# A gated linear attention block: the part of the state carried in as quarter-array products added in PSUM, and x normalised and turned a tile ahead

## The reference

```python
h = layernorm(x) * (1 + ca) + sa
q, k, v = h @ Wq.T, h @ Wk.T, h @ Wv.T          # 16 heads of 64
log_decay = -softplus(h @ Wd.T + bd)            # one number a token and head
k = k * sigmoid(h @ Wg.T)
s_t = exp(log_decay_t) * s_{t-1} + k_t^T v_t ;  o_t = q_t s_t
x = x + ga * (rmsnorm(o) * norm_w * sigmoid(h @ Wog.T)) @ Wo.T
h = layernorm(x) * (1 + cb) + sb
x = x + gb * ffn(h)                             # token shift, sigmoid(r) * (relu(k)^2 @ Wv)
```

## Time and profile before

| | us |
|---|---|
| median of 3 runs | 3521.03 |
| lowest, highest | 3518.96, 3521.23 |
| the profiled execution | 3524.34 |
| its span in the trace | 3522.6 |
| PE busy in it | 3429.8 (97%) |
| DVE, ACT, POOL busy | 1938.0, 1235.5, 436.6 |
| first pass, from the first transposes of x to the last sum o | 43.5 to 2181.4 |

### The profile page before, as it was taken

The page is one execution under the profiler, slowest core; times in us unless marked ns, Lnnn a source line. Parts: engine busy times, 40 slices in busy tenths (PEclk is TensorE's granted clock), DMA queues, the critical chain, the costliest instruction groups (busy, mean ns, idle before and its releaser), DMA issues. The chain is left out here.

```text
span 3522.6 us, 83072 instructions
## 1 busy us (share of the span) xinstructions
PE 3429.8 (97%) x30085; PEld 3140.0 (89%) x30085; DVE 1938.0 (55%) x4693; ACT 1235.5 (35%) x3072; POOL 436.6 (12%) x723
## 2 busy tenths in 40 slices
PE   7999999999999999999999997899999999999998
PEld 7999999999999999999999996799989899899987
DVE  4444444444444444444444444667677766767676
ACT  4334334333333333333333332332333333233332
POOL 0110110110110110110110111212111111112110
PEclk8999999999999999999999997899999999999999
DMA  4333332332332333333333324422221122212220
GB/s 146 94 95 74 99 91 74 102 87 75 104 85 75 106 83 76 106 82 76 105 82 80 103 75 126 147 72 82 77 91 71 71 83 91 76 71 77 77 95 24
DMA packets 243936, 309.08 MB, mean 88 GB/s; under 512 B 22160, under 2 KB 188064, under 8 KB 239792
## 3 DMA queue, kind: packets, MB, share of 16 engines
q1 hardware_dynamic: 243888, 308.42, 29.7%
HBM read 223.40 MB, written 84.93 MB: 88 GB/s over the span
## 5 line engine op out<-in xcount | busy, mean ns | idle before, releaser
L730 DVE SCALAR_TENSOR_TENSOR mid<-state,w_cur,psQ 64x64 f32<-64x64 f32 x512 | 143.4, 280 | 686.0 <-PE psQ L525 682.3
L627 ACT ACTIVATE prob<-cum_rows,w_cur 128x128 f32<-128x128 f32 x1024 | 327.4, 393 | 132.2 <-POOL cum_rows L808 105.0
L55 PE MATMUL psJ<-h_hi,w_g_hi 128*128 128x256 f32 x1024 | 311.0, 304 | 21.7 <-DVE h_lo L686 20.9
L55 PE MATMUL psJ<-h_hi,w_q_hi 128*128 128x256 f32 x1024 | 303.9, 297 | 0.0
L607 ACT COPY q<-psJ 128x256 f32<-128x256 f32 x256 | 95.8, 374 | 586.6 <-PE psJ L57 586.6
L55 PE MATMUL psG<-h_hi,w_og_hi 128*128 128x256 f32 x1024 | 287.1, 280 | 7.0 <-DMA h_lo<-h_dram 7.0
L56 PE MATMUL psJ<-h_lo,w_q_hi 128*128 128x256 f32 x1024 | 285.4, 279 | 0.0
L56 PE MATMUL psJ<-h_lo,w_g_hi 128*128 128x256 f32 x1024 | 285.3, 279 | 0.0
L57 PE MATMUL psJ<-h_hi,w_g_lo 128*128 128x256 f32 x1024 | 284.7, 278 | 0.0
L55 PE MATMUL psJ<-h_hi,w_k_hi 128*128 128x256 f32 x1024 | 284.0, 277 | 0.7 <-ACT w_new L613 0.7
L57 PE MATMUL psJ<-h_hi,w_q_lo 128*128 128x256 f32 x1024 | 284.6, 278 | 0.0
(11 more groups left out here) (214 smaller groups left out, 9656.8 us busy)
## 6 DMA issues: line engine op xcount, KB each, us to landing
cum_rows<-cum_dram SPq DMA_DIRECT2D x256, 256.0 KB, 5.6
grown<-cum_dram SPq DMA_DIRECT2D x512, 64.0 KB, 3.4
o_dram<-o SPq DMA_DIRECT2D x256, 128.0 KB, 1.9
o_cols<-o_dram SPq DMA_DIRECT2D x32, 1024.0 KB, 5.9
an_norm_x<-in_L_attn_x_dram SPq DMA_DIRECT2D x32, 512.0 KB, 3.5
h_dram<-h_hi SPq DMA_DIRECT2D x32, 512.0 KB, 4.0
h_dram<-h_lo SPq DMA_DIRECT2D x32, 512.0 KB, 5.2
h_hi<-h_dram SPq DMA_DIRECT2D x32, 512.0 KB, 3.9
```

The lines of the kernel that those rows point to most:

```text
L55: nc.tensor.matmul(out, w_hi, x_hi, start=first, stop=False)
L627: last = nc.scalar.activation(prob[:, p % 2, 2 * h + c, :], cum_rows[:, p % 4, 2 * c + h, :], ACT.Exp, bias=w_cur[:, 0, c, 2 * p + h:2 * p ...
L730: last = nc.vector.scalar_tensor_tensor(out=mid[r, r], in0=state[r, p, r], scalar=w_cur[r, 3, 0, 2 * p + h:2 * p + h + 1], in1=psK[r, 0, r ...
```

## The change

The output of a pair is now summed in PSUM. `grow_q` (DVE) multiplies q with `grown` before the product, `weigh_v` opens the sum with prob times v, and `add_held`, one step later, adds the products of the grown q with the state before the first chunk (`held`, a copy by ACT) and with `mid`, in four matmuls of 64x64 quarters of the array. The full-array products with state and mid, `inter` and the sum `add_o` are gone; ACT copies the finished o out of PSUM (`copy_o`). State and mid are 128x64, and DVE updates each in one instruction with one scalar a row (`w_all`). In psO the two chunks of a pair lie crosswise over the partitions, so o is stored with four DMAs of 64x128 in place of one of 128x256. psK moved into the bank of the scores and psN into psO's.

x is loaded in step 1 for two tiles ahead, normalised in steps 4 and 5 of the tile before, turned in step 1 (before the pair's k), and scaled in step 2; `rest_h` makes its four pieces in a row. The loop over tiles is one tile shorter, with that tile written out.

```diff
-        state = sb("state", [P, NP, P])
-        mid = sb("mid", [P, P])
+        state = sb("state", [P, NP, DH])
+        held = sb("held", [P, 2, DH])
+        mid = sb("mid", [P, 2, DH])
-        inter = sb("inter", [P, NC, CH])
+        qg = sb("qg", [P, 2, T])
...
-        psS, psX, psN = psB[:, :, 0:2, :], psB[:, 0, 2:4, :], psB[0:2 * NC * H, 1, 2, :]
-        psQ = ps("psQ", [P, 4, CH])
-        psI, psK = psQ[:, 0:2, :], psQ[:, 2:4, :]
-        psO = ps("psO", [P, 4, CH])[:, 0:NC, :]
+        psS, psX, psK = psB[:, :, 0:2, :], psB[:, 0, 2:4, :], psB[:, 1, 2:4, 0:DH]
+        psP = ps("psP", [P, 2, 4, CH])
+        psO, psN = psP[:, :, 0, :], psP[0:2 * NC * H, 0, 1, :]
...
         def grow_rows(sp, i, p):
-            hold(sp, s["inter"], NP * i + p - 1)
+            hold(sp, s["qg"], NP * i + p - 1)
...
         def sp_tile(sp, i, gla, proj, prep):
             j = i - 1
-            if prep:
-                hold(sp, s["xT"], KD * (i + 1))
-                sp.dma_start(x[:, :, :], x_v[i + 1]).then_inc(s["x"], 16)
             for p in range(NP):
+                if p == 1 and prep > 1:
+                    sp.wait_ge(s["xT"], KD * (i + 2))
+                    sp.dma_start(x[:, :, :], x_v[i + 2]).then_inc(s["x"], 16)
...
                     sp.wait_ge(s["o"], NP * j + p + 1)
-                    sp.dma_start(o_v[j, :, p, :, :], o[:, p % 2, :, :]).then_inc(store[p % 2], 16)
+                    for h in range(2):
+                        for side in range(2):
+                            sp.dma_start(o_v[j, h * DH:(h + 1) * DH, p, (h + side) % 2, :],
+                                         o[side * DH:(side + 1) * DH, p % 2, h, :]).then_inc(store[p % 2], 16)
...
         def weigh_v(pe, n, p):
             pe.wait_ge(s["prob"], n + 1)
+            pe.wait_ge(s["mid"], n + 1)
+            pe.wait_ge(s["held"], n + 1)
+            pe.wait_ge(s["qg"], n + 1)
             hold(pe, s["o"], n)
...
+                    side = (h + c) % 2
+                    nc.tensor.matmul(psO[side * DH:(side + 1) * DH, h, :], v[:, c, p * P + h * DH:p * P + (h + 1) * DH],
+                                     prob[:, p % 2, 2 * h + c, :], start=True, stop=False, tile_position=(0, side * DH))
+
+        def add_held(pe, p):
+            for c, s_in in enumerate((held, mid)):
+                for h in range(2):
+                    r, side = slice(h * DH, (h + 1) * DH), (h + c) % 2
+                    last = nc.tensor.matmul(psO[side * DH:(side + 1) * DH, h, :], s_in[r, p % 2, :],
+                                            qg[r, p % 2, c * CH:(c + 1) * CH], start=False, stop=True,
+                                            tile_position=(h * DH, side * DH))
             last.then_inc(s["gla"], 1)
...
+                if p == (1 if gla else 4) and prep:
+                    turn_x(pe, i + 1)
...
-                    nc.tensor.matmul(psI[:, 0, :], state[:, p, :], q[:, p, 0:CH], start=True,
-                                     stop=True).then_inc(s["held"], 1)
+                    if p > 0 or not opens:
+                        add_held(pe, (p - 1) % NP)
...
-                if gla:
-                    pe.wait_ge(s["state"], n + 1)
...
-                    nc.tensor.matmul(psI[:, 1, :], mid[:, :], q[:, p, CH:T], start=True,
-                                     stop=True).then_inc(s["ready"], 1)
...
-                if p == 6 and prep:
-                    turn_x(pe, i + 1)
...
+        def keep_state(act, j, p):
+            n = NP * j + p
+            hold(act, s["state"], n + 1 - NP)
+            hold(act, s["gla"], n - 1)
+            nc.scalar.copy(held[:, p % 2, :], state[:, p, :]).then_inc(s["held"], 1)
+
+        def copy_o(act, n, p, j):
+            act.wait_ge(s["gla"], n + 1)
+            hold(act, store[p % 2], 64 * (NP // 2 * j + p // 2))
+            nc.scalar.copy(o[:, p % 2, :, :], psO[:, :, :]).then_inc(s["o"], 1)
...
-                if p == 7 and prep:
+                if p == (2 if gla else 5) and prep:
                     affine_h(act, i + 1)
...
-        def add_o(dve, n, p, j):
-            dve.wait_ge(s["gla"], n + 1)
-            dve.wait_ge(s["inter"], n + 1)
-            hold(dve, store[p % 2], 16 * (NP // 2 * j + p // 2))
-            nc.vector.tensor_tensor(o[:, p % 2, :, :], inter[:, :, :], psO[:, :, :], ALU.add).then_inc(s["o"], 1)
+        def grow_q(dve, j, p):
+            n = NP * j + p
+            dve.wait_ge(s["by_act"], act_done(j, ("q", p)))
+            dve.wait_ge(grow[p % 2], 32 * (NP // 2 * j + p // 2 + 1))
+            hold(dve, s["gla"], n - 1)
+            nc.vector.tensor_tensor(qg[:, p % 2, :], q[:, p, :], grown[:, p % 2, :, :].rearrange("p c t -> p (c t)"),
+                                    ALU.mult).then_inc(s["qg"], 1)
...
+                    grow_q(dve, j, p)
+                    dve.wait_ge(s["score"], n + 1)
                     dve.wait_ge(s["held"], n + 1)
...
+                    nc.vector.scalar_tensor_tensor(out=mid[:, p % 2, :], in0=state[:, p, :], scalar=w_all[:, 0, p:p + 1],
+                                                   in1=psK[:, 0, :], op0=ALU.mult, op1=ALU.add).then_inc(s["mid"], 1)
                     dve.wait_ge(s["mid"], n + 1)
...
-                    for k in range(2 if gla else KD):
+                    for k in range(KD):
                         rest_h(dve, i, k)
...
-                if p == 4 and prep:
-                    norm_stats(dve, i + 1)
-                if p == 5 and prep:
-                    norm_x(dve, i + 1)
+                if p == 4 and prep > 1:
+                    norm_stats(dve, i + 2)
+                if p == 5 and prep > 1:
+                    norm_x(dve, i + 2)
```

More of the change, by code:

```diff
@@ L360, in attention_pass @@
         s = signals(nc, ctx, "a", "xT hT h_hi h_lo h_kept zb softin e1 l soft g_raw cum w_new n_turned n_out n_rows "
-                 "cur proj by_act k e mask score prob kT kw inc mid state held ready gla inter o zero")
+                 "cur proj by_act k e mask score prob kT kw inc mid state held qg gla o zero")
         s.update(norm["s"])
@@ L430, in _ @@
         def _(sp):
[L431 to L436, removed]
+            sp.wait_ge(s["xT"], KD)
+            sp.dma_start(x[:, :, :], x_v[1]).then_inc(s["x"], 16)
+            sp_tile(sp, 0, False, True, 2)
+            sp_tile(sp, 1, True, True, 2)
+            with sp.Fori(2, NT - 2) as i:
+                sp_tile(sp, i, True, True, 2)
+            sp_tile(sp, NT - 2, True, True, 1)
+            sp_tile(sp, NT - 1, True, True, 0)
+            sp_tile(sp, NT, True, False, 0)
             for n in range(2):
-                sp.wait_ge(store[n], 16 * NP // 2 * NT)
+                sp.wait_ge(store[n], 64 * NP // 2 * NT)
             sp.wait_ge(s["h_kept"], 32 * NT)
@@ L474, in weigh_v @@
                 for h in range(2):
-                    last = nc.tensor.matmul(psO[h * DH:(h + 1) * DH, c, :],
-                                            v[:, c, p * P + h * DH:p * P + (h + 1) * DH],
-                                            prob[:, p % 2, 2 * h + c, :], start=True, stop=True,
-                                            tile_position=(0, h * DH))
+                    side = (h + c) % 2
[8 more added lines that the diff above has]
+                                            tile_position=(h * DH, side * DH))
             last.then_inc(s["gla"], 1)
@@ L504, in pe_tile @@
                     if p > 0 or not opens:
+                        if p == 7 and proj:
+                            pe.wait_ge(s["n_out"], i + 1)
                         weigh_v(pe, n - 1, (p - 1) % NP)
                     pe.wait_ge(s["kw"], n + 1)
-                    hold(pe, s["inter"], n)
+                    hold(pe, s["state"], n)
                     pe.wait_ge(s["by_act"], act_done(j, ("q", p)))
@@ L512, in pe_tile @@
                             r = slice(h * DH, (h + 1) * DH)
-                            last = nc.tensor.matmul(psK[r, c, r], kw[:, c, r],
+                            last = nc.tensor.matmul(psK[r, c, :], kw[:, c, r],
                                                     v[:, c, p * P + h * DH:p * P + (h + 1) * DH],
@@ L554, in _ @@
             turn_x(pe, 0)
-            pe_tile(pe, 0, False, True, True)
-            pe_tile(pe, 1, True, True, True, True)
-            with pe.Fori(2, NT - 1) as i:
-                pe_tile(pe, i, True, True, True)
-            pe_tile(pe, NT - 1, True, True, False)
-            pe_tile(pe, NT, True, False, False)
+            pe_tile(pe, 0, False, True, 2)
+            pe_tile(pe, 1, True, True, 2, True)
+            with pe.Fori(2, NT - 2) as i:
+                pe_tile(pe, i, True, True, 2)
+            pe_tile(pe, NT - 2, True, True, 1)
+            pe_tile(pe, NT - 1, True, True, 0)
+            pe_tile(pe, NT, True, False, 0)
             weigh_v(pe, NP * NT - 1, NP - 1)
+            add_held(pe, NP - 1)
         def affine_h(act, n):
@@ L633, in act_tile @@
                         copy_v(act, j, 5)
+                if p > 0 and proj:
```

(17 more changed lines are left out.)

96 lines of the change are left out of this document (35 added, 61 removed).

## The result

The changed kernel takes 3545.72 us (median of four runs, 3543.55 to 3548.66) against 3521.03 us before (also of four runs). The ratio is 1.0072, interval [1.0055, 1.0089]: it is slower, by 25 us or 0.7%, where 3455 us was forecast. The profiled execution lasted 3546.25 us.

A forecast was written before the change was run, and what follows sets the result against it. PE, busy 97% of the span, was taken as the bound. From 3524.3 us, 88 gained and 24 lost on pair 3's late rows gave 3460, 3457 after the profiled run's 3.3 us offset, stated as 3455 us, range 3425 to 3505.

The forecast's parts named there:

- terms 1 and 2: On PE, dropping the product with mid gains 47.7 us; four quarter products for the full state product gain 5 us.
- the late third block: At the turn of a tile, the g projection's third block no longer waits for h's rounding: 9.0 us gained.
- terms 3 and 4: Transposes of x moved into step 1's wait gain 26.4 us; h's four low parts in a row gain 9.0 us.
- What comes on ACT and DVE, at nothing: ACT's copies of state and o, some 0.6 us a step, and DVE's grow_q are covered by those engines' slack.
- The chain: Sum, copy, stores, grown loads, grow_q, prob, then PE's turning of k: 0.5 us to spare, tight in pairs 2, 3, 6.
- Four stores at the pace of store to load, 0.52: On SP's queue, the four stores of o take the chain from S + 0.63 to S + 2.7.
- S + 0.63: When o reaches the store; S is the start of a q projection, where the sum of the pair before closes.
- Pair 3: Its grown rows queue behind x on SP: 1.3 us of transfer less 0.5 slack, 0.8 us a tile, 24 us lost.
- The grown rows become the bound: Rival: 64-row stores issue in 0.8, not 0.52; pairs 2 and 6 are 1.1 late, pair 3 2.4; 3576 us, chance 0.09.
- Quarters two by two: Rival: the four quarter products on PE run in pairs, 0.25 us more a step; 3517 us, chance 0.10.
- the signs named for being wrong: PE idle over 1 us ahead of k's transposes in several steps, four stores issuing over 2.6 us, or add_held over 0.4 us.

The follow-up runs named there:

- e5: e1 with the load, normalising, turning and scaling of x put back where the kernel before has them: 3463.65 us, ratio 0.9836.
- e6: Kernel before with only x a tile further ahead and inter behind the four low parts of h; products and stores as before: 3512.54 us, ratio 0.9971.
- e10: e1 with grow_q moved behind prob on DVE: 3434.49 us, ratio 0.9751 against the kernel before.
- e3: Changed kernel with the load of x issued in step 3 in place of step 1, behind the grown rows of pairs 3 and 4: 3515.91 us.
- e1: Changed kernel with the two loads of grown for pair p + 2 issued ahead of the wait for o and its four stores: 3436.14 us.
- e9: Changed kernel with only pair 3's two loads of grown issued ahead of the wait for o and the four stores: 3495.28 us.
- e8: Changed kernel with two stores of 128x128 in place of four of 64x128, chunks in the wrong places in DRAM: 3448.56 us.

## Why the prediction was wrong

By its own steps:

- **The product with mid, and the quarters for the state (terms 1 and 2, 53 us): right.** e5 has 58. Its 31 full tiles, from the first transposes of k to those of the last tile, take 1989.5 us and not 2040.4, which is 51 of the 58; 5.9 more come in the last tile (35.3 us against 41.2 up to step 7's transposes of k), where 2 were forecast. Scores with the four quarters took 0.82, the forecast's sum. The rule of 60 cycles a matmul in the Trainium skill (TensorEngine Tiling (Array Packing), section Instruction Overhead), taken as a cost added by each, would have made it 25 us less good, and e5's 58 us exclude that.
- **x ahead and the late third block (terms 3 and 4, 35 us): nearly right**, 27.5. In the 31 tiles it is 32.4 us (1989.5 to 1957.1); 3.7 are lost again ahead of them, where the first tiles wait for the second x (the first transposes of k start at 93.83 and not 90.11). The first g projection starts 0.31 behind the first transpose of k, not 0.22. By e6, 17 us of these terms hold only because psN changed its bank, which the prediction didn't price.
- **What comes on ACT and DVE, at nothing: right.** e10 has PE busy all the time with all of it in place.
- **The chain: right as a mechanism, wrong by its sizes.** It was followed link by link, its slack put at 0.5 us, and pairs 2, 3 and 6 named as the tight ones. Three links measured otherwise for pair 2 in the tile shown. The four stores take 2.67 us to the next issue and not 2.08: this is the step that failed first, and for every pair. *"Four stores at the pace of store to load, 0.52"* took the pace from a store of 128 rows, and stores of 64 rows go at 0.67. The loads need 4.45 us from their first issue to qg, where 4.2 was counted. And o reaches the queue at S + 0.75 instead of S + 0.63. That is 0.96 us more; DVE's part is 0.07 shorter (qg to k 1.68), and the slack was 0.5, which leaves 0.39. PE itself came 0.08 earlier than forecast (S + 9.07), so k starts 0.48 later than it could; 0.32 of that is counted as idle, as the modelled end of the matmul before covers 0.16.
- **Pair 3: a term was missing.** Only x's bytes were added to it (0.8 us). But all of SyncE's issues of a step stand in one queue, and between pair 0's stores and pair 1's they make 7.7 us in a step of 6.2: four stores, two loads, two stores of h, x and one row load. That puts 1.6 us on pair 3's stores ahead of any transfer. The stores themselves take 2.80 and not 2.08, the loads 5.13 up to qg and not 4.2; with the slack, DVE's 0.07 and the 0.48 by which pair 2 has already made the step longer, k starts 2.25 us late, 2.09 of it idle. Of the 7.7, the prediction named each in its text, and summed none but the stores and loads of one pair. A queue's issues have to be added up over the step like the work of an engine. This missing term cost the most: 58.4 us in the 31 tiles, 1.9 each, against 8.6 in front of step 3, 0.3 each. Moved out of that queue, x gave back 30 us (e3); four stores made one gave back 105 (e2), as that shortens both.
- **The sum**: of the 84.1 us of PE's wait for prob 66 lie in the 31 tiles and 18 in the last tile. The profiled executions of the changed kernel and e1 are 110.5 us apart. The 31 tiles take 2056.6 us and 1957.1, 99.5 more: PE idles 68.7 us in them and 1.1, the clock costs 18.8 us and 0, and 45 waits at the 0.16 that the idle time leaves out make 7. The last tile's steps take 44.5 us and 34.5, 10 more; the prediction had them 2 us shorter than before (41.2). So 103 of the 110.5 are placed. The fall of the clock behind a 2 us wait had no place in any case of the prediction, though the earlier trace rows showed the lower level in a stretch with waits.
- **The rivals.** *The grown rows become the bound* was the one that happened, given 0.09. It put pairs 2 and 6 at 1.1 and pair 3 at 2.4 late, 4.6 us a tile in all, for 3576. Measured are 0.3 a tile for pair 2, none for pair 6 and 1.9 for pair 3 (idle time), and the clock: 3546. Its condition, stores as slow to issue as the loads of 64 rows (0.8), holds about half: 0.67. The argument against it (loads that spread a row differ from plain stores) was no measurement; the trace had no store of 64 rows, the two nearest rows were 0.52 and 0.8, and with a slack of 0.5 us against four such steps the value between them decided the sign. *Quarters two by two* did not occur. The other rule of the Trainium skill (DMA: Bandwidth & Descriptors, queues, rings and completion order) fits e9, where the longest landing of a load of grown rows was 6.9 us and pair 3's stood behind x and h in the tile shown; no run tells order in the ring from shared bandwidth.
- Of the signs named for being wrong, the four stores took 2.48 and 2.62 us to issue in the tile shown, where 2.6 was the bound, and idle time of over 1 us stood ahead of k's transposes in one step a tile and not in several. Both pointed at the right place, and neither was passed clearly.

## What to carry to other kernels

Before a DMA is split, add up what its queue issues in one step of the loop, every transfer of it, and compare that with the step; a queue that is full between two of its waits is an engine at its bound, though no table of busy time lists it. Put loads that something waits for ahead of stores that nobody waits for, and on the engine that consumes them put that consumer behind what the critical engine waits for. When a slack is a sum of many terms and a fraction of one of them would turn the sign, give the case in which it does a chance to match, and not one in ten.

## What the runs showed of the hardware

- Issuing a DMA from SyncE costs by its rows in a way I did not expect: 128 rows of 1 KB or of 512 B 0.34 us (medians 346 and 338 ns), 64 rows of 512 B 0.49 us (median 494 ns). Half the rows took longer. The loads of 64 rows took longer too: a median of 607 ns before the change and 671 after.
- A DMA's time to issue depends on what was issued just before: the rows of a pair (256 KB) take 0.40 us by themselves, 0.52 behind the two stores of h (e3) and 1.09 behind the stores of h and the load of x. In e3 the rows are quicker but the four stores behind them take 3.11 us in place of 2.62. Why isn't shown.
- Waits of about 2 us of PE in a stretch that is otherwise full can bring the granted clock from 1.00 to 0.50 for 3.4 us. From 200 to 2000 us of the changed kernel this happened in 10 of the 26 tiles with a wait of over 1 us in step 4; those waits were 1.9 to 3.0 us long, those of the other 16 tiles 1.3 to 2.6. So a wait's length alone doesn't tell. e9 has one such stretch from 200 to 2000 us, behind a wait of 1.9 us; e3, with waits of up to 1.4, and e8, with up to 0.8, have none.
